# Expert tiles with the first product made transposed and its weights loaded per tile, and a new split of the second sort's scatters

## What is computed

```python
gate_logits = x @ gate_w + gate_b
topk_vals, topk_idx = jax.lax.top_k(gate_logits, 2)            # 16 experts
topk_w = jax.nn.softmax(topk_vals, axis=-1)
h = jax.nn.relu(jnp.einsum('bsh,ehf->bsef', x, w1) + b1)        # 256 -> 512
expert_out = jnp.einsum('bsef,efh->bseh', h, w2) + b2           # 512 -> 256
moe = jnp.sum(topk_w[..., None] * chosen(expert_out, topk_idx), axis=2)
```

## Time and profile before

| | us |
|---|---|
| median of 3 runs | 3290.81 (3286.86 to 3295.12) |
| the profiled execution | 3285.42, its span 3283.7 |
| busy over the span: PE, DVE, ACT, POOL | 1682.9, 1903.3, 801.3, 1842.5 |
| DMA moved | 224.80 MB, mean 68 GB/s |
| tile loop's first product, L1391 | 256 matmuls, mean 625 ns |
| second product, L1407 | 512 matmuls, mean 382 ns |
| scatters of the second sort, L230 | 391, mean 970 ns |

### The profile page before, as it was taken

One profiled execution on the slowest core, in us unless ns is written; L12 is line 12 of the kernel. 1 busy time (PEld: TensorE's weight loads), 2 busy tenths in 40 slices (PEclk: granted clock), 3 DMA queues, 4 the chain that ended last, 5 costly groups with the idle time before them and its releaser, 6 DMA issues. The chain is left out here.

```text
span 3283.7 us, 53507 instructions
## 1 busy us (share of the span) xinstructions
PE 1682.9 (51%) x12473; PEld 1234.2 (38%) x12474; DVE 1903.3 (58%) x5554; ACT 801.3 (24%) x2540; POOL 1842.5 (56%) x1834
## 2 busy tenths in 40 slices
PE   0487443056667665059990028752444444430697
PEld 0254332044445444036660016531444334320465
DVE  5775997087777766212220372377777777655422
ACT  0143110044444431013330013200233333220122
POOL 0577777677777770577777547203777777720000
PEclk9998665578887865579995558875666655665799
DMA  3200000153333371433331210104444434763100
GB/s 113 88 22 15 1 2 1 54 163 106 106 106 105 106 89 12 158 77 87 86 81 32 54 29 21 18 0 86 106 105 106 104 105 105 91 49 81 29 16 23
DMA packets 177667, 224.80 MB, mean 68 GB/s; under 512 B 85419, under 2 KB 137136, under 8 KB 177479
## 3 DMA queue, kind: packets, MB, share of 16 engines
q0 software_dynamic: 82752, 139.83, 19.9%
q1 hardware_dynamic: 94852, 84.30, 9.0%
HBM read 185.01 MB, written 38.87 MB: 68 GB/s over the span
## 5 line engine op out<-in xcount | busy, mean ns | idle before, releaser
L2057 POOL DMA_INDIRECT e_rows<-mid_table,e_rec x488 | 488.6, 1001 | 328.5 <-DVE e_same L2169 179.5
L230 POOL DMA_INDIRECT mid_sorted<-p_record,p_row x391 | 406.5, 1040 | 226.3 <-issue 123.0
L852 POOL DMA_INDIRECT e_rows<-mid_table,e_rec x448 | 433.4, 967 | 157.7 <-issue 96.0
L230 POOL DMA_INDIRECT mid_sorted<-keep_record,keep_row x391 | 379.4, 970 | 125.3 <-issue 125.3
L1012 PE MATMUL e_ps_A<-e_rows,e_hot 128*125 128x260 f32 x896 | 331.5, 505 | 0.0
L2313 PE MATMUL e_ps_mT<-keep_ident,e_marked 128*128 128x128 f32 x488 | 118.3, 423 | 196.1 <-DVE e_marked L2081 196.1
L1012 PEld LDWEIGHTS e_ps_A<-e_rows,e_hot 128*125 128x125 f32 x896 | 202.2, 250 | 28.2
L2275 ACT ACTIVATE e_acc<-e_state 128x66 f32 x488 | 126.1, 258 | 259.5 <-ACT e_acc L2275 212.5
L997 PE MATMUL e_ps_T<-e_identb,e_hot 128*125 128x128 bf16 x454 | 89.4, 289 | 191.1 <-DVE e_hot L873 189.2
L1366 DVE COPY x_hidden<-x_ps_h 128x512 f32<-128x512 f32 x64 | 44.3, 692 | 244.0 <-PE x_ps_h L1391 244.0
L2313 PEld LDWEIGHTS e_ps_mT<-keep_ident,e_marked 128*128 128x128 f32 x488 | 95.6, 223 | 200.6 <-issue 200.6
(11 more groups left out here) (516 smaller groups left out, 4102.9 us busy)
## 6 DMA issues: line engine op xcount, KB each, us to landing
e_rows<-mid_table,e_rec POOLq DMA_INDIRECT x936
mid_expert_in<-p_zrow SPq DMA_DIRECT2D x1, 8192.0 KB, 29.5
w<-in_L_ffn_w SPq DMA_DIRECT2D x16, 512.0 KB
x_w<-in_L_ffn_w SPq DMA_DIRECT2D x16, 512.0 KB
x_xs<-mid_expert_in SPq DMA_DIRECT2D x64, 128.0 KB
x_b<-in_L_ffn_b SPq DMA_DIRECT2D x64, 128.0 KB
mid_expert_out<-x_y SPq DMA_DIRECT2D x64, 128.0 KB
mid_sorted<-p_record,p_row POOLq DMA_INDIRECT x391
```

Of the source, the lines that this page charges most:

```text
L230: pool.indirect_dma_start(out=to, out_offset=bass.IndirectOffsetOnAxis(ap=row[:, t:t + 1].bitcast(U32), axis=0), in_=record[:, t, :], in_o ...
L852: pool.indirect_dma_start(out=rows[:, s % RING * 2 + j, :], out_offset=None, in_=k["table"], in_offset=bass.IndirectOffsetOnAxis(ap=rec[:, ...
L2057: pool.indirect_dma_start(out=rows[:, j, q, :], out_offset=None, in_=k["table1"], in_offset=bass.IndirectOffsetOnAxis(ap=rec[:, i * TG + q ...
```

## The change

The first product of a tile is computed transposed: the weights are the stationary operand and xT streams, 128 columns at a time, so 8 products (in two passes each) write the transposed hidden rows directly. The transposes `turn_h`, the buffers `hidden` and `ps_h` and VectorE's copy go; hT gets two buffers. The first weights are no longer loaded ahead in `stage_edges0` but by SP for each tile, between the reading of the expert and the load of xs, into a ring of four with one semaphore each. PE's `first_product` no longer reads the expert; it waits for the weights, for xT, and for ACT to have kept hT of tile s-2. In PE's iteration `turn_x(s + 2)` moves ahead of `second_product(s)`. ACT makes hT of tile s+1 instead of s, with a wait for the second product of tile s-1. 180 scatters of the second sort are issued in `stage_experts` instead of 272, and 211 in `stage_project1` instead of 119.

```diff
--- before
+++ after
@@
-SCATTERS_EARLY = 272
+SCATTERS_EARLY = 180
@@ stage_edges0, SP's program
-            for e in range(E0):
-                load_weight(sp, k["w1"][:, e], a["L0_ffn_w1"][e], s_w1)
-            sp.wait_ge(s_w1, 16 * E0)
@@ stage_experts, buffers
         RING = 4
+        w1 = m.sb("w1", [P, RING, DC, F0])
         xs = m.sb("xs", [P, RING, D])
         xT = m.sb("xT", [P, 2, DC, P])
-        hidden = m.sb("hidden", [P, F0])
-        hT = m.sb("hT", [P, FC, P])
+        hT = m.sb("hT", [P, 2, FC, P])
...
-        ps_h = [m.ps(f"ps_h{i}", [P, F0]) for i in range(2)]
         ps_hT = [m.ps(f"ps_hT{i}", [P, FC, P]) for i in range(2)]
@@ SP, step
                 e = expert(sp, s)
+                load_weight(sp, w1[:, q], a["L0_ffn_w1"][bass.ds(e, 1)].rearrange("a d f -> (a d) f"), s_w1[q])
                 sp.dma_start(xs[:, q, :], ...
@@ ACT
-            def step(s, q, i):
+            def keep_h(s, q):
                 e = expert(act, s)
+                if after(s, 2):
+                    wait_alone(act, s_y, s - 1)
                 wait_alone(act, s_hT, s + 1)
                 for c in range(FC):
-                    last = nc.scalar.activation(hT[:, c, :], ps_hT[q % 2][:, c, :], ACT.Relu, bias=k["b1T"][:, bass.ds(e * FC + c, 1)])
+                    last = nc.scalar.activation(hT[:, q % 2, c, :], ps_hT[q % 2][:, c, :], ACT.Relu, bias=k["b1T"][:, bass.ds(e * FC + c, 1)])
                 last.then_inc(s_hTk, 1)
-                if before(s + 2, X_N):
-                    keep_x(s + 2, q)
+            def step(s, q, i):
+                if before(s + 1, X_N):
+                    keep_h(s + 1, q + 1)
+                if before(s + 2, X_N):
+                    keep_x(s + 2, q)
             keep_x(0, 0)
             keep_x(1, 1)
+            keep_h(0, 0)
             turns(act, step)
@@ VectorE
-            def keep_h(s, q):
-                dve.wait_ge(s_h, s + 1)
-                nc.vector.tensor_copy(hidden[:], ps_h[q % 2][:]).then_inc(s_hk, 1)
...
@@ PE
-            def first_product(s, q):
-                e = expert(pe, s)
+            def first_product(s, q, i):
+                wait_alone(pe, s_w1[q % RING], (i + q // RING) * 16 + 16)
                 wait_alone(pe, s_xTk, s + 1)
-                for c in range(DC):
-                    last = nc.tensor.matmul(ps_h[q % 2][:], xT[:, q % 2, c, :], k["w1"][:, bass.ds(e, 1), c, :].rearrange("p a f -> p (a f)"),
-                                            start=c == 0, stop=c == DC - 1)
-                last.then_inc(s_h, 1)
-            def turn_h(s, q):
-                wait_alone(pe, s_hk, s + 1)
-                for c in range(FC):
-                    last = nc.tensor.transpose(ps_hT[q % 2][:, c, :], hidden[:, c * P:(c + 1) * P], k["ident"][:])
+                if after(s, 2):
+                    wait_alone(pe, s_hTk, s - 1)
+                for f in range(FC):
+                    for c in range(DC):
+                        last = nc.tensor.matmul(ps_hT[q % 2][:, f, :], w1[:, q % RING, c, f * P:(f + 1) * P],
+                                                xT[:, q % 2, c, :], start=c == 0, stop=c == DC - 1)
                 last.then_inc(s_hT, 1)
...
             def step(s, q, i):
                 if before(s + 1, X_N):
-                    first_product(s + 1, q + 1)
-                second_product(s, q)
+                    first_product(s + 1, q + 1, i)
                 if before(s + 2, X_N):
                     turn_x(s + 2, (q + 2) % RING, i + (q + 2) // RING)
-                if before(s + 1, X_N):
-                    turn_h(s + 1, q + 1)
+                second_product(s, q)
@@ build: the [P, E0, DC, F0] tensor "w1" around three stages goes
```

More of the change, by code:

```diff
@@ L808, in stage_edges0 @@
         s_in = m.sem("in")
-        s_w1 = m.sem("expert_weights")
         s_const = m.sem("const_ready")
@@ L1269, in stage_experts @@
         s_xs = [m.sem(f"tile_in{i}") for i in range(RING)]
+        s_w1 = [m.sem(f"first_weights{i}") for i in range(RING)]
         s_xT = m.sem("xT_made")
         s_xTk = m.sem("xT_kept")
-        s_h = m.sem("hidden_made")
-        s_hk = m.sem("hidden_kept")
         s_hT = m.sem("hidden_T_made")
@@ L1363, in _ @@
         def _(dve):
-            def keep_h(s, q):
-                dve.wait_ge(s_h, s + 1)
-                nc.vector.tensor_copy(hidden[:], ps_h[q % 2][:]).then_inc(s_hk, 1)
             def step(s, q, i):
-                if before(s + 1, X_N):
-                    keep_h(s + 1, q + 1)
                 if after(s, 2):
@@ L1374, in step @@
                 nc.vector.tensor_tensor(y[:, q % 2, :], ps_y[q % 2][:], b2[:, q, :], ALU.add).then_inc(s_yk, 1)
-            keep_h(0, 0)
             turns(dve, step)
@@ L1406, in second_product @@
                 for c in range(FC):
-                    last = nc.tensor.matmul(ps_y[q % 2][:], hT[:, c, :], w2[:, bass.ds(e, 1), c, :].rearrange("p a d -> p (a d)"),
+                    last = nc.tensor.matmul(ps_y[q % 2][:], hT[:, q % 2, c, :], w2[:, bass.ds(e, 1), c, :].rearrange("p a d -> p (a d)"),
                                             start=c == 0, stop=c == FC - 1)
@@ L1422, in _ @@
             pe.wait_ge(s_w2, 16 * E0)
-            first_product(0, 0)
-            turn_h(0, 0)
+            first_product(0, 0, 0)
             turns(pe, step)
@@ L2717, in build @@
             k["normed"] = k["acc0"][:, :, 0:D]
[L2718 to L2721, removed]
+            stage_edges0(nc, a, k)
+            stage_gate(nc, a, k)
+            stage_experts(nc, a, k)
             stage_combine(nc, a, k)
```

## The result

The changed kernel took 3267.72 us (median of 4 runs, 3267.01 to 3272.24) against 3290.31 us for the kernel before (4 runs): ratio 0.9933, 95% interval 0.9916 to 0.995, that is 22.6 us less. The forecast was 3251, some 40 less.

The account below looks back on a forecast made before the run. After POOL's scatters, a two-tile load round trip would bound the expert stage: 0.62 + 1.45 + 4.8 + 2.56 = 9.43 us. Over 30 pairs 39.3 us gained, plus 1 in the edge stage: 3290.8 - 40 = 3251, range 3206 to 3290.

Parts of the forecast that it names:

- What bounds the stage: Expert stage: POOL's scatters bound it before, with 42 us of slack in the tile loop; the loop bounds it after.
- 92 more scatters in the projection are free: Projection stage: 92 more scatters take 121 us, landing by 2210 against the stage's end at 2257, so cost nothing.
- Rival 4: Projection stage: VectorE's work blocks POOL, ending the stage 71 us late, 3322 us in all; chance 0.04.
- PE's own work, 3.95 us a tile: Expert tile loop: PE alone would do a tile in 3.95 us after the change, against 4.62 before.
- Rival 1: Expert tile loop: the round trip is no limit and PE sets the pace, gain 86 us, 3205 us; chance 0.14.
- The round trip bounds the loop: Expert tile loop: second product, y, SP's loads, landing, transposes, second product take 9.43 us per two tiles.
- Weights' issue to all landed, 4.8 us: Expert tile loop: from the weights' issue until all loads have landed 4.8 us, with 4.5 and 6.8 also derived.
- rival 2: Expert tile loop: queueing of stores and loads makes landing 6 to 6.8 us, 3295 us in all; chance 0.12.
- transposes to the end of the second product: Expert tile loop, on PE: 2.56 us, including 0.48 of idle for reading the expert's number; 2.05 without it.
- the sum: Expert stage: first tiles, 30 pairs at 9.43 us, last three tiles and ending put the next stage 39.3 us earlier.
- rival 3: Expert tile loop: PE's stops lower its clock to 0.81, pair 11.1 us, 3301 us in all; chance 0.07.
- First edge stage: First edge stage: removing 16 weight loads that crowd a load VectorE waits for gains 1 us, bounds 0 and 3.

Follow-up runs that it names:

- Experiment 9: Kernel before with only the scatter split changed, 180 early instead of 272, old tiles kept: 3248.9 us, ratio 0.9892 to the kernel before.
- experiment 10: Changed kernel with the early scatters set back to 272, so the new tiles alone: 3284.56 us, ratio 0.9997 to the kernel before.
- experiment 5: Changed kernel with a ring of eight tiles instead of four for weights, rows and bias: 3196.2 us, ratio 0.9729 to the kernel before.
- 7: Changed kernel with ring of eight, early read of the expert's number, and weights' load behind rows and bias: 3192.47 us, ratio 0.9718 to the kernel before.
- 12: Changed kernel with a ring of eight for rows and bias, four for the weights: 3196.25 us, ratio 0.973 to the kernel before.
- experiment 11: Changed kernel with PE's read of the expert's number moved ahead of the waits: 3236.74 us, ratio 0.9853 to the kernel before.
- experiment 3: Changed kernel with the weights' load behind the rows' and bias's, on another, slower chip: 4350.58 us, ratio 1.0027 to the kernel before there.
- 2: Changed kernel with 272 early scatters, so the new tiles alone, on another, slower chip: 4371.02 us, ratio 1.0073 to the kernel before there.
- 8: Changed kernel, ring of four, with early read of the expert's number and weights' load behind rows and bias: 3232.13 us, ratio 0.984 to the kernel before.

## Why the prediction was right, and where it was off

- **What bounds the stage.** Right: POOL's scatters before, the loop after. Experiment 9 shows this part alone as -36 us; 10 shows that without it the rest brings nothing.
- **92 more scatters in the projection are free.** Right: 93 of them stand in its second part in 122 us (2063 to the last one's end at 2185.2), 1.31 each as forecast, 53 us before the stage's end, beside 75.5 us of VectorE. Rival 4 (POOL blocked for all of VectorE's time) is out. The Trainium skill ("GPSIMD Engine Reference", "Specifications") has VectorE instructions with two SBUF inputs contend with GpSimd. The trace agrees: nine scatters of this stage take 1.67 to 2.04 us, all others 0.96 to 1.20, and each of the nine runs beside a VectorE instruction of 1.5 us with two inputs in SBUF, as here:

```profile
2170.21 1.49 DVE L1792 TENSOR_TENSOR keep_x<-keep_x,acc  x1 [0.20 <-DVE acc L1788]
2170.49 2.04 POOL L230 DMA_INDIRECT mid_sorted<-keep_record,keep_row  x1 [0.30 <-issue]
```

The nine cost 8 us in all over 211 scatters, about what parts 1.32 us from one scatter's start to the next in this stage from 1.28 in the expert stage. Other such VectorE instructions of 1.5 us left the scatters beside them at 0.96 to 1.20. So the rival was wrong in how often POOL is held up, not in that it is.

- **PE's own work, 3.95 us a tile.** 3.87 measured, in experiments 5, 7 and 12, with the sixteen weight loads of the first product in 1.86 us. Rival 1's time (3205) was close for what it supposed, 3196, but in the changed kernel its condition doesn't hold.
- **The round trip bounds the loop.** Right in mechanism: experiment 5 lengthens the lead and changes nothing else, 12 lengthens it for the rows and the bias alone, and 65 and 62 us of the expert stage go.
- **Weights' issue to all landed, 4.8 us**, for which the bounds lay furthest apart. It was 0.57 + 0.52 + 3.76 = 4.85 to the first transpose, and 4.6 to the landing by the semaphore. The row of the same load was the one to take; rival 2 (6 us and more) is out. The Trainium skill ("DMA: Bandwidth & Descriptors", "Anatomy of one DMA") would have it at 3.8 for the 768 KB; its fit is made for DMAs issued from GpSimd, and these are issued from SP. The measurement decides.
- **The term that was mis-sized: transposes to the end of the second product.** The prediction took 2.56 us, 0.48 of it the read of the expert, from one tile at the start of the old loop. There four transposes had started just before, and the 0.48 (a gap between weight loads) is only what was left of the read behind them:

```profile
1433.22 0.63 PE L1398 MATMUL x_ps_hT<-keep_ident,x_hidden 128*128 128x128 f32 x4 [0.88 <-DVE x_hidden L1366]
```

From the first of them to the next product, at 1434.10, it is 0.88 us. In the changed kernel two transposes lie over the read, and it is 1.06. The term measured 1.06 + 1.83 = 2.89 instead of 2.56. That is 0.33 us a pair, nearly the whole difference between 9.43 and 9.78, and over 30 pairs that difference is 10.5 of the 14.7 us by which the stage came out longer than forecast (408.7 against 394.0). The range for this term ended at the value chosen, so it had no room above.

- **The rest, some 4 us,** is in the first pairs: two tiles there have a pitch of 7.4 us (y to y), while the sum let every pair be the same. No run took these apart.
- **The clock.** It stayed at 0.99 in the loop (1440 to 1730) with PE idle 17% of the time in short stops, the longest of PE's waits listed above 1.8 us; rival 3 is out.
- **First edge stage.** Forecast 1 us. The small load that VectorE waits for took 4.64 us (5.18 in experiment 10) instead of 5.74 (5.70 in experiment 9, which keeps the old loads): 0.5 to 1.1 us.

Taken together, the change is a gain of 36 us from one number and a loss from the new tiles, 14 us by the ratios (0.9933 against 0.9892) and 18 by the expert stage (408.7 against 390.7). A longer lead for 256 KB a tile turns that loss into a gain of 53 (0.973 against 0.9892).

## What to carry to other kernels

When a wait on a load moves ahead of work whose result frees the buffer, write the loop from buffer to buffer and add its terms: it can bound the kernel while every engine and the queues have room, and the cure is a longer lead for whatever closes the loop, here four tiles more for the small loads and not for the large one. Reads of registers that are free while an engine's program runs ahead of its work are charged in full just behind a wait, so they belong ahead of it. Of two edits shipped as one, time each alone: here one number held the whole gain.

## What the runs showed that was not expected

- A read of an index from memory on PE, with a wait just ahead of it and two transposes queued, leaves PE idle for 0.7 us (48 waits of 0.69 us in the mean, 0.86 in the tile shown); put ahead of the wait, it is not seen (experiment 11).
- On the second chip the other engines hardly advance while POOL issues indirect scatters (50 us a tile instead of 4.62), and the whole is 32% longer, though POOL issues them at the same pace (1.27 us each, 1.28 on the first). There, moving them from one cover to another was worth nothing (0.9999).
- 512 KB going ahead delay the bias' landing by 0.4 us, but the rows' by 1.5 or more: with the weights ahead, the first 16 of a tile's 32 updates have come only 3.6 us after the rows' issue, against 2.06 without. The bias lands last in either case: as many bytes as the rows, but one row of 1 KB put into all partitions, and 3.06 us from its issue where the rows take 2.06. It closes the loop; a quicker way to load it was not tried.
- A bias sent 0.56 us sooner, with the weights behind it, landed 0.4 to 0.5 us later after its issue (experiment 3 against 2, 8 against 11). Why was not taken apart.
